# Other slots for the mixing and the embeddings of later batches in the attention pipeline of a two-layer network, with new order tables for both halves

## What is computed

```python
# x: 8 batches x 512 tokens x 128
xn = layernorm(x)
s = window_attention_block(xn)         # windows of 10 and 20 tokens, projections, small FFN
g = silu(mixture_of_experts(xn))       # 8 experts, top 2, and a shared one
x = x + s * g                          # end of the first half; "mix" in the kernel
xn = layernorm(x)
# second half: attention over 512 tokens, 16 heads of 8
q_mag, k_mag = softplus(q), softplus(k)            # "embed" in the kernel
q_embed = [q_mag * cos(pos), q_mag * sin(pos)]
k_embed = [k_mag * cos(pos + bias), k_mag * sin(pos + bias)]
attn = softmax(q_embed @ k_embed.T / sqrt(8));  s = attn @ v @ wo.T
g = silu(mixture_of_experts_2(rmsnorm(xn)))        # 8 experts, top 2, width 352
x = x + s * g                                      # "mix1"
```

## Time and profile before

| | |
|---|---|
| median of 3 runs | 1364.43 us (1363.96 to 1365.02) |
| profiled execution | 1360.38 us |
| its span, first to last instruction | 1358.6 us |
| mean granted TensorE clock | 0.839 of full speed |
| busy: TensorE, VectorE, ScalarE, GpSimd | 71%, 66%, 50%, 44% of the span |
| chain that ended last | TensorE 30%, VectorE 11%, ScalarE 8%, DMA 5% of the span |

### The profile page before, as it was taken

How to read it: one execution, slowest core, us unless ns; L and a number is a source line. 1 busy time by engine, 2 the same in 40 slices (tenths; PEclk the granted TensorE clock), 3 DMA queues, 4 the chain that set the end, 5 groups by cost and what they waited for, 6 DMA issues and landing times.

```text
span 1358.6 us, 16130 instructions
## 1 busy us (share of the span) xinstructions
PE 970.4 (71%) x5318; PEld 521.5 (38%) x5318; DVE 899.0 (66%) x1366; ACT 677.4 (50%) x1009; POOL 593.5 (44%) x585
## 2 busy tenths in 40 slices
PE   5464466877777624377667778778999987677784
PEld 5221234544444312133222223226888852223231
DVE  6572766565666545968888865755666677876861
ACT  3221245454554332357667466664344346566674
POOL 6377545677784164453711456650000034706210
PEclk7776688788887865569788798978999998899999
DMA  7713445545565119224213352635655633544400
GB/s 244 260 43 110 136 102 154 154 131 157 145 161 144 64 34 115 35 41 67 43 23 48 53 95 45 113 85 124 212 192 193 205 74 67 88 62 63 72 21 13
DMA packets 86481, 142.11 MB, mean 105 GB/s; under 512 B 14973, under 2 KB 43774, under 8 KB 86398
## 3 DMA queue, kind: packets, MB, share of 16 engines
q1 hardware_dynamic: 77726, 123.50, 37.8%
q0 software_dynamic: 8192, 16.79, 5.0%
q10 hardware_dynamic: 480, 0.79, 0.5%
HBM read 58.17 MB, written 40.37 MB: 73 GB/s over the span
## 4 chain that ended last, share of the span: by engine, by line
PE 30%; DVE 11%; ACT 8%; DMA 5%; issue 4%; SPq 4%; POOL 3%; DVEq 0%; ACTq 0%; POOLq 0%
PE PS L915 7%; PE PS L874 5%; ACT P L982 5%; PE PS L934 5%; PE PS L892 4%; SPq L495 4%; DMA KS<-MAG 3%; PE PS L854 3%; DVE MX L1721 2%; PE PS L840 2%; DVE XNT L1462 2%; POOL A L1298 2%; PE PS L674 1%; PE PS L679 1%; ACT MAG L982 1%
## 5 line engine op out<-in xcount | busy, mean ns | idle before, releaser
L1721 DVE TENSOR_REDUCE MX<-PS 128x2 f32<-128x1024 f32 x256 | 306.5, 1222 | 123.4 <-PE PS L854 117.8
L982 ACT ACTIVATE P<-PS 128x1024 f32<-128x1024 f32 x256 | 262.4, 1025 | 168.4 <-PE PS L892 163.6
L854 PE MATMUL PS<-KS,QS 62*128 62x512 f32 x512 | 140.4, 546 | 69.7 <-DVE MX L1721 54.9
L1298 POOL DMA_INDIRECT A<-Y1D,POS x64 | 62.2, 972 | 273.4 <-DMA Y1D<-YE 186.7
L892 PE MATMUL PS<-QS,KS 64*128 64x512 f32 x512 | 125.9, 488 | 71.5 <-ACT P L982 68.9
L874 PE MATMUL PS<-P,V 128*32 128x512 f32 x1024 | 156.3, 686 | 0.1
L854 PEld LDWEIGHTS PS<-KS,QS 62*128 62x128 f32 x512 | 54.2, 209 | 211.3 <-DVE MX L1721 112.3
L915 PE MATMUL PS<-XRH,WH 128*128 128x512 f32 (+1 forms) x276 | 104.1, 419 | 0.0
L892 PEld LDWEIGHTS PS<-QS,KS 64*128 64x128 f32 x512 | 54.0, 206 | 122.7 <-ACT P L982 113.6
L773 PE MATMUL PS<-XST,WB 128*128 128x512 f32 x184 | 99.5, 683 | 0.0
L1317 POOL DMA_INDIRECT XS1D<-XN,POS x64 | 62.3, 973 | 63.2 <-DVE MX L1721 40.4
(11 more groups left out here) (220 smaller groups left out, 1854.8 us busy)
## 6 DMA issues: line engine op xcount, KB each, us to landing
WH<-W1SD SPq DMA_DIRECT2D x23, 704.0 KB, 4.8
WS<-WD SPq DMA_DIRECT2D x64, 200.0 KB, 4.2
QS<-EH SPq DMA_DIRECT2D x64, 128.0 KB, 4.3
KS<-EH SPq DMA_DIRECT2D x60, 128.0 KB, 5.8
WB<-in_wb SPq DMA_DIRECT2D x23, 322.0 KB, 2.9
XS<-XS0D SPq DMA_DIRECT2D x23, 256.0 KB, 4.2
Y0D<-YE SPq DMA_DIRECT2D x23, 256.0 KB, 4.3
XS<-XS1D SPq DMA_DIRECT2D x23, 256.0 KB, 3.8
```

The costliest lines, as they stand in the source:

```text
L854: signal(pe.matmul(PS[:, s % 4, :], QS[rows, u % 3, hp, 128 * t:128 * t + 128], KS[rows, u % 3, hp, :], start=True, stop=True), "ms")
L982: act.activation(*a, **k).then_inc(sem[name], 1)
L1298: pool.indirect_dma_start(dst[:, k, t, :], None, src, bass.IndirectOffsetOnAxis(pos[:, k, g:g + 1], 0)).then_inc(sem[name], 16)
L1721: go("mx", dve.tensor_reduce(MX[:, u % 2, t].rearrange("p (o h) -> p o h", o=2)[:, :, hp], PS[:, s % 4 - 1:s % 4 + 1, :], AX.X, ALU.max))
```

## The change

Two tables replace the formulas that place the mixing and the embeddings, and `MOVED` and `MOVED1` get other values. No instruction is added, removed or resized; the engines' lists hold the same items in another order. In the second half the lists of all engines but SyncE change.

```diff
-STEP1 = 10
-ROUTE_AT = 7 * STEP1 + 8
+MIX_AT = (0, 4, 19, 33, 43, 46, 59, 65)
+EMBED_AT = (0, 14, 42, 77, 108, 138, 170, 202)
+ROUTE_AT = 78
...
     for b in range(1, B):
-        at = 1 if b == 1 else STEP1 * b - 1
+        at = MIX_AT[b]
         put(at, ("sum", b))
         put(at + 1, ("mix", b), ("stats", b))
...
-    embed(6, 1)
-    put(5, ("v", 1), ("vev", 1))
+    embed(EMBED_AT[1], 1)
+    put(MIX_AT[1] + 4, ("v", 1), ("vev", 1))
     put(16, ("stack", 2))
     for b in range(2, B):
-        embed(32 * b - 20, b)
+        embed(EMBED_AT[b], b)
         put(32 * b - 9, ("v", b), ("vev", b))
```

More of the change, by code:

```diff
@@ L60 @@
 LEAD = 20
-STEP1 = 10
-ROUTE_AT = 7 * STEP1 + 8
+MIX_AT = (0, 4, 19, 33, 43, 46, 59, 65)
+EMBED_AT = (0, 14, 42, 77, 108, 138, 170, 202)
+ROUTE_AT = 78
 SEND_AT = ROUTE_AT + ROUTE_PARTS + 1
 BLOCKS_AT = SEND_AT + 72
-MOVED = {'POOL': {('window', 11): 0.1, 'send': -5.1, ('tail', 2): 1.0, ('qk', 6): -0.6, 'sub1': -1, ('qk', 5): -1, 'split': 3.5, 'mul0': 0.3, ('qk', 2): 1.3, ('less', 0): 1.1, 'mul1': -1.1, ('tail', 3): 0.1, ('even', 0): -0.9, ('less', 1): -1.3}, 'DVE': {('less', 0): 0.9, ('even', 0): 0.6, ('even', 1): 0.3, ('tail', 1): 0.7, 'yev': 1.4, ('window', 14): -1.5, ('qk', 9): 1.5, ('window', 18): 0.1, ('qk', 6): 0.4, ('window', 11): 1.0, ('qk', 8): 0.1, ('qk', 7): 0.3, ('window', 20): -0.6, 'clip': 0.1, 'act': 0.4, ('window', 13): 0.6, ('window', 10): -0.5, ('window', 7): -0.4, 'mul0': 1.5, ('qk', 0): 1.5, ('qk', 2): -0.3, ('less', 1): -1}, 'PE': {'down_e': 1.7, ('tail', 6): -1, ('window', 10): 1.5, ('tail', 7): -0.8, ('window', 8): 0.8, 'sorted': -3.0, ('tail', 1): -0.6, ('tail', 0): -0.7, ('tail', 4): 0.5, ('pair', 1): 1, ('window', 4): -0.4, ('window', 3): -0.1, ('window', 6): 0.1}, 'ACT': {('tail', 6): -1, ('tail', 2): 0.3, ('window', 3): 0.8, 'split': -2.3, 'sorted': -2.6, ('window', 12): 0.4, 'silu': 1, ('gate', 0): -0.4, ('tail', 5): -0.5, ('tail', 0): -0.6, ('tail', 4): -0.3}, 'plan': {'period': 9, 'step': 3, 'start': 1}, 'SP': {('window', 14): 2.1, ('pair', 0): 2.2, 'yev': 5.5, 'split': 5.4}}
@@ new lines @@
+MOVED = {'POOL': {('window', 11): 0.1, 'send': -4.1, ('tail', 2): 1.0, ('qk', 6): -0.6, 'sub1': -1, ('qk', 5): -1, 'split': 3.5, 'mul0': 0.3, ('qk', 2): 1.3, ('less', 0): 1.1, 'mul1': -1.1, ('tail', 3): 0.1, ('even', 0): -0.9, ('less', 1): -1.3, ('qk', 1): -0.6, ('even', 1): -0.3}, 'DVE': {('less', 0): 0.9, ('even', 0): 0.6, ('even', 1): 0.3, ('tail', 1): 1.0, 'yev': 1.4, ('window', 14): -1.5, ('qk', 9): 1.5, ('window', 18): 0.1, ('qk', 6): 0.4, ('window', 11): 1.0, ('qk', 8): 0.1, ('qk', 7): 0.3, ('window', 20): -0.6, 'act': 0.4, ('window', 13): 0.6, ('window', 10): -0.5, ('window', 7): -0.4, 'mul0': 1.5, ('qk', 0): 1.5, ('qk', 2): 1.2, ('less', 1): -1, ('tail', 3): -0.6, ('window', 9): -0.6}, 'PE': {'down_e': 1.4, ('tail', 6): -1, ('window', 10): 1.8, ('tail', 7): -0.8, ('window', 8): 0.8, 'sorted': -3.0, ('tail', 1): -0.6, ('tail', 0): -0.7, ('tail', 4): 0.2, ('pair', 1): 1, ('window', 4): -0.4, ('window', 3): -0.1, ('window', 6): 0.1}, 'ACT': {('tail', 6): -1, ('tail', 2): 0.3, ('window', 3): 0.8, 'split': -2.3, 'sorted': -2.6, ('window', 12): 0.4, 'silu': 1, ('gate', 0): -0.4, ('tail', 5): -0.5, ('tail', 0): -0.7}, 'plan': {'period': 9, 'step': 3, 'start': 1}, 'SP': {('window', 14): 2.7, ('pair', 0): 2.2, 'yev': 5.5, 'split': 5.4}}
@@ L115, in plan0 @@
     return out + [item for _, item in sorted(timed, key=lambda t: t[0])]
-MOVED1 = {'DVE': {'norm_first': -1.5, 'hilo': 1.7, 'mix1': 2.1, 'sum_first': -3.1, 'mix_first': -3.0, 'stats_first': -2.5, 'mag': 0.2, 'sum': 3, 'logitsev': 1.5, 'mix1_first': -8, 'stats': 3, 'sum1_first': -0.1, 'ot_first': 0.1, 'route_first': -0.6, 'max_first': 3, 'hilo_first': 0.1, 'route': 1}, 'POOL': {'stats_first': -1.0, 'hilo_first': 1.7, 'hilo': 4.0, 'get1': -0.9, 'get_first': -6.7, 'send': 1.7, 'get': -0.3, 'get1_first': 1.4, 'stats': 2, 'mag_first': 0.9, 'mag': -2}, 'ACT': {'qkev_first': 0.7, 'sum1': 2.0, 'sum_first': -2.2, 'ln': 0.5, 'vev_first': 0.9, 'ln_first': -1.5, 'exp_first': 0.4, 'sum': 1.5, 'sum1_first': 2, 'woev': 1, 'qkev': 0.1, 'route_first': -0.6}, 'PE': {'qk_first': 0.6, 'max_first': -0.4, 'norm': -1.4, 'turn': 0.1, 'logits_first': 0.1, 'v_first': 0.3, 'qk': 0.5, 'logits': -1.5, 'wo_first': 0.3, 'oq_first': 0.1, 'route_first': -0.6, 'route': 1}, 'SP': {'mix1_first': 2.4, 'mix1': 1.7, 'minus': 3.4, 'stack': -1, 'minus_first': -2.9, 'stack_first': 1}}
+MOVED1 = {'DVE': {'norm_first': -1.5, 'hilo': 1.7, 'mix1': 2.4, 'sum_first': -4.6, 'mix_first': -3.0, 'stats_first': -2.2, 'mag': 0.2, 'sum': 3, 'logitsev': 0.5, 'mix1_first': -8.1, 'sum1_first': -0.1, 'route_first': -2.6, 'max_first': 2, 'hilo_first': 0.2, 'norm': 0.6, 'ot': 0.6, 'mag_first': -1, 'mix': -0.3, 'ot_first': 0.3}, 'POOL': {'stats_first': -1.0, 'hilo': 2.0, 'get1': -2.4, 'get_first': -3.7, 'send': 2.1, 'get1_first': 6.4, 'stats': -1.6, 'mag': -0.1, 'send_first': 0.1, 'mix1_first': -1.6, 'mix1': 2}, 'ACT': {'qkev_first': 0.8, 'sum1': 1.4, 'sum_first': -2.2, 'ln': -1.0, 'vev_first': 0.9, 'ln_first': -1.5, 'exp_first': 0.4, 'sum': 1.5, 'sum1_first': 2, 'woev': 2, 'qkev': 0.1, 'route_first': -2.6, 'normev': -3, 'outev_first': 1.5, 'route': 0.3}, 'PE': {'qk_first': 0.6, 'norm': -0.8, 'turn': -0.9, 'logits_first': 0.1, 'v_first': 0.3, 'qk': 0.5, 'logits': -0.6, 'wo_first': 0.3, 'oq_first': 0.1, 'route_first': -3.2, 'out': 0.1, 'oq': 0.6}, 'SP': {'mix1_first': 4.0, 'mix1': 1.4, 'stack': -2.5, 'minus_first': -2.4, 'minus': -1.1}}
 def plan1(engine):
```

## The result

The change makes the kernel slower. Its median is 1384.55 us (1380.66 to 1385.96, 4 runs), against 1364.20 (1359.38 to 1365.02, 4 runs) for the kernel before in the same comparison: a ratio of 1.0177 [1.0141, 1.0214]. The forecast was 1351, its range ended at 1364. The profiled execution took 1385.96 us (span 1384.2), 25.6 more than the one of before.

The account below looks back on a forecast made before the run. VectorE was taken to bound the second half, its stops beside GpSimd (34.4 us) paid almost one to one. Terms -1.7 -4.4 -0.5 +0 -6.8 = -13.4 us, from 1364.43 to 1351; range 1335 to 1364.

Parts of the forecast that it names:

- Part F: First half: order only, one expert matmul group one place earlier and small shifts; 0, -2.4 to +2.4 us.
- Part A: Second half, slots 0 to 32: `sum` 2 and `mix` 2 escape GpSimd's stops, less some new costs; -1.7 us.
- near tie of `norm` 2: Slots 0 to 32: `norm` 2 starts close to `mag` 1, half its instructions taken as caught; +4.8 us (0 to 7.9).
- Part B: Slots 38 to 60: `norm` 5 and `sum` 6 partly escape GpSimd's work on batch 2; -4.4 us.
- The other near tie: Slots 38 to 60: `norm` 5 moves close to the start of `mag` 2, half still caught; -7.9 +4.8 us.
- The wait for the stack of unit 3: Slots 38 to 60: projections two slots earlier may wait for this stack; +1.0 us (0 to 3.9).
- The rule weighed: Shared VectorE-GpSimd pair: whoever issues first holds it; if VectorE does, both 4.8 us terms vanish, giving 1341.
- Part C: Routing and batch 3: routing ends before `mag` 3, less waits for the prefix product and a stack; -0.5 us.
- Part D: Batches 4 and 5: batch 5's earlier projections wait for stack 9, absorbed later; 0 us (-3 to +3.9).
- Part E: From 1098 us, batches 6 and 7: `sum1` 2 mostly escapes `mag` 6 and the last chain shortens; -6.8 us.
- the wait ahead of batch 7: ScalarE's wait for stack 13 grows but the chain to stack 14 shortens; -2.0 us (-3.9 to +3.9).
- rival 3: Earlier embeddings at slots 42, 138, 170 and 202 wait for the previous batch's stacks; slower, 1372 us; 10%.

Follow-up runs that it names:

- e3_pe: Kernel before with only TensorE's new first-half order entries (down_e ahead of the last window product, once per batch): 1.0243, +33 us.
- e10_fill: e3_pe with most idle time ahead of the up projection filled by repeated transposes: 1.0104 against the kernel before, +14 us.
- e13_late: e1_second with the order entries for items behind the expert blocks as before: 0.9983 against the kernel before, -2 us.
- e5_embed: Kernel before with only the embeddings of batches 5, 6 and 7 moved to slots 138, 170 and 202: 0.9967, -4.5 us.
- e1_second: Changed kernel with MOVED put back, so only the second half of the change: 0.9978 against the kernel before, -3 us.
- e12_hybrid5: Kernel before with the change's second-half places and entries ahead of the expert blocks, and norm 5 ahead of the 47th maximum: 0.9936, -9 us.
- e9_split: Kernel before with four of down_e's eight matmuls ahead of the last window product and four behind, in all batches: 1.0172, +23 us.

## Why the prediction was wrong, step by step

- **Part F, the step that failed.** It put the first half at 0 +- 2.4 us and took the bound from a single wait. I had read the exchange of `down_e` and the last window product from the lists ("one matmul group of the experts one place earlier"), but priced it once and not once per batch, and did not ask who waits for the item that was passed. The rows were in reach: VectorE already waited 0.54 us for the head sum (290.08), GpSimd and ScalarE wait behind it in turn, and behind them stands TensorE's own next work. What the runs showed in its place: e3_pe, with this exchange alone, loses 33 us in the comparison and 27.4 by the first maximum of its trace. Five of the eight batches pay, about 5 us each in the kernel after; 2.08 us of delay in each of them would be 10, and e10_fill shows that 3 to 4 us a batch are matmuls at the low clock. The bound had been taken from another wait.
- **Part A**: -7.0 against -1.7. The stops of `sum` 2 and `mix` 2 (10.5 us) went as said. The term mis-sized is the near tie of `norm` 2, priced at half (4.8): with 1.15 us of margin it came out free, and the sum without it is -6.5.
- **Part B**: -1.9 against -4.4. The other near tie, also priced at half, was lost in full (9.76 us), so -7.9 +4.8 became +0.8 instead of -3.1. `sum` 6 gained 3.1 us (predicted 2.3). The wait for the stack of unit 3, taken at 1.0, was 3.37 us (651.48). On another chip the tie fell the other way (e13_late).
- **The rule weighed.** VectorE's record begins 0.03 us ahead of GpSimd's and still shows four instructions in 9.76 us, so, if the records' starts give the order of issue, coming first did not save it. `norm` 2 does not test the rule: it had ended before `mag` 1 began. The 1341 of that rule did not come.
- **Part C**: +2.0 against -0.5. Routing escaped only in part: `mag` 3 still meets the last steps, two of them taking 2.06 and 2.00 us at 770.50 and 773.51, where 3.6 us were to go.
- **Part D**: right at 0. The wait for stack 9 grew from 2.92 to 6.25 us, maximum 157 came 2.4 us later than before (counted from maximum 96), and maximum 158, behind the blocks, 0.8 us earlier: the loss came back over the blocks, as the part argued.
- **Part E**: +6.2 against -6.8. `sum1` 2 was freed, 2.00 us. The term mis-sized is the wait ahead of batch 7, taken at -2.0: the stretch around it (maxima 200 to 208) grew by 7.4 us, of which 2.2 came back. That is rival 3's mechanism at one of its four places; alone (e5_embed) it costs 4.4 there, and the stretch behind the blocks is not longer for it. What makes the difference stays open.
- **The sum**: A to E were predicted at -13.4 and gave -0.8 in the trace, +0.9 with the end behind the last maximum, -3 in the comparison of e1_second. Without part F the time would have been about 1361.

## What to carry to other kernels

When an order table changes, look on an in-order engine for the item that was passed, and price every exchange by the number of rounds in which it happens: if a chain over several engines hangs on that item, its delay can be paid in each round, and the time it used to hide under is opened as idle time. Check which clock TensorE has behind each wait of a loop: where it already drops in every second round, a wait of one or two microseconds more can make it drop in all. The two near ties between VectorE and GpSimd here were not half a loss each: one cost nothing, the other all four instructions, and that one fell differently on another chip. So give a near tie margin in the list.

## What the runs showed of the hardware

A loop can sit in a steady pattern of two rounds, one with QKV at 1.60 us and one at 2.93, with an average that hides it; the same lists can also leave that pattern (e5_embed, e12_hybrid5). After a projection at the low clock, a wait of 0.95 us ahead of the up projection left the following matmuls at 2.4 GHz (before, 295.20). In e3_pe and e9_split the clock had come back, and behind a wait of 2.27 us they ran at 1.2 (305.10, 335.12). In the kernel after waits of 0.79 and 1.42 us, with only transposes between, left them at 1.2 as well (306.94). Filling the wait of 2.27 us with 16 useless transposes made the kernel with the exchange faster, by 11 to 17 us in four batches. And the same kernel took 1361 to 1364 us on some chips and 1444 to 1448 on two others.
